# Cross-attention and gated feed-forward on one core: K's stacked rows laid out for two batches, and another ending for the last batch

## The reference

```python
x = x + attention(layernorm(x), ctx)     # 16 heads of depth 16, biases,
                                         # scores * 16**-0.5 / temperature[head], softmax
h = silu(n @ wg.T) * (n @ wu.T)          # n = layernorm(x), 768 hidden, int weights / 127
x = x + h @ wd.T
```

## Time and profile before

| | |
|---|---|
| runs | 410.18, 410.93 and 411.25 us, median 410.93 |
| the profiled execution | 409.33 us, of which 407.6 us are its span |
| busy | TensorE 89%, its weight loads 80%, VectorE 73%, ScalarE 63%, GpSimd 39% |
| mean granted TensorE clock | 0.975 |
| DMA packets | 61749, 34049 of them under 512 B; 37.68 MB |

### The profile page before, as it was taken

One profiled execution on the slowest core, in us unless ns is written; L12 is line 12 of the kernel. 1 busy time (PEld: TensorE's weight loads), 2 busy tenths in 40 slices (PEclk: granted clock), 3 DMA queues, 4 the chain that ended last, 5 costly groups with the idle time before them and its releaser, 6 DMA issues.

```text
span 407.6 us, 9738 instructions
## 1 busy us (share of the span) xinstructions
PE 363.9 (89%) x3398; PEld 326.9 (80%) x3398; DVE 298.2 (73%) x734; ACT 256.2 (63%) x564; POOL 158.7 (39%) x282
## 2 busy tenths in 40 slices
PE   0567578799999999999999999999998999998984
PEld 0566465688999899989999898999997988787984
DVE  6974657678878877787788778888777686745743
ACT  2353366577776767676777686767766675756442
POOL 3133313264434443343426263626353061613322
PEclk9979689999999999999999999999999999999989
DMA  6999595536523753184525591739137622010000
GB/s 174 294 101 155 76 157 88 87 76 123 101 65 77 141 118 78 33 161 110 112 58 89 124 157 32 141 53 159 26 84 83 113 31 81 15 42 2 27 27 27
DMA packets 61749, 37.68 MB, mean 92 GB/s; under 512 B 34049, under 2 KB 61185, under 8 KB 61697
## 3 DMA queue, kind: packets, MB, share of 16 engines
q1 hardware_dynamic: 61696, 36.99, 47.4%
HBM read 14.04 MB, written 4.19 MB: 45 GB/s over the span
## 4 chain that ended last, share of the span: by engine, by line
PE 67%; DMA 11%; SPq 6%; DVE 5%; ACT 4%; issue 3%; POOL 3%; ACTq 0%; DVEq 0%
PE ps_w L807 28%; DMA qs<-q 9%; PE ps_w L800 9%; PE ps_o L936 6%; PE ps_b L920 6%; PE ps_a L910 6%; SPq L395 5%; PE ps_w L792 5%; PE ps_w L819 4%; PE ps_w L840 3%; DMA ks<-k 1%; ACT probs L545 1%; DVE ks L695 1%; POOL hidT L463 1%; DMA probs<-wkT 1%
## 5 line engine op out<-in xcount | busy, mean ns | idle before, releaser
L463 POOL TENSOR_TENSOR hidT<-hid,hidT 128x256 fp32r<-128x256 f32 x80 | 58.9, 738 | 124.7 <-ACT hidT L538 124.7
L807 PE MATMUL ps_w<-xn2T,wg 128*128 128x256 f32 x384 | 103.0, 301 | 0.2 <-DVE xn2T L632 0.2
L807 PE MATMUL ps_w<-xn2T,wu 128*128 128x256 f32 x384 | 96.2, 282 | 0.0
L545 ACT ACTIVATE probs<-ps_b 120x512 f32<-120x512 f32 x128 | 76.0, 593 | 22.8 <-PE ps_b L920 22.5
L710 DVE TENSOR_REDUCE negmax<-ps_a 128x4 f32<-128x480 f32 x128 | 82.8, 648 | 8.7 <-PE ps_a L910 8.4
L807 PEld LDWEIGHTS ps_w<-xn2T,wg 128*128 128x128 f32 x384 | 72.9, 190 | 1.5 <-issue 0.5
L807 PEld LDWEIGHTS ps_w<-xn2T,wu 128*128 128x128 f32 x384 | 73.1, 190 | 0.0
L910 PE MATMUL ps_a<-ks,qs 96*128 96x120 bf16 x512 | 49.9, 222 | 12.0 <-DMA qs<-q 7.5
L556 ACT ACTIVATE tanh_g<-ps_w 128x256 f32<-128x256 f32 x96 | 36.8, 383 | 37.2 <-PE ps_w L807 35.9
L807 PE MATMUL ps_w<-wd,hidT 128*128 128x256 f32 x384 | 55.8, 293 | 3.0 <-POOL hidT L463 2.6
L920 PE MATMUL ps_b<-qs,ks 98*120 98x256 bf16 x256 | 50.6, 279 | 4.6 <-ACT probs L545 3.2
(11 more groups left out here) (93 smaller groups left out, 602.9 us busy)
## 6 DMA issues: line engine op xcount, KB each, us to landing
qs<-q SPq DMA_DIRECT2D x96, 128.0 KB, 4.5
ks<-k SPq DMA_DIRECT2D x96, 60.0 KB, 2.6
x_tok<-x SPq DMA_DIRECT2D x16, 256.0 KB, 4.5
x_res<-x SPq DMA_DIRECT2D x16, 256.0 KB, 4.6
out<-y SPq DMA_DIRECT2D x16, 256.0 KB, 2.5
ctx_raw<-ctx SPq DMA_DIRECT2D x16, 120.0 KB, 4.3
y<-wgT SPq DMA_DIRECT2D x2, 384.0 KB, 5.7
x<-wuT SPq DMA_DIRECT2D x2, 384.0 KB, 6.7
```

Of the source, the lines that this page charges most:

```text
L463: nc.gpsimd.tensor_tensor(hidT[:, 1, f], hid[:, f % 2], hidT[:, 0, f].bitcast(F32), ALU.subtract).then_inc(hid_lo, 1)
L545: nc.scalar.activation(probs[0:NKV, e % PROBS], ps_b[0:NKV], ACT.Exp).then_inc(exp_done, 1)
L807: last = nc.tensor.matmul(dst, lhsT, rhs, start=(start and k == 0), stop=(stop and k == len(terms) - 1), skip_group_check=True)
```

## The change

`ks` becomes two buffers, each for two batches side by side, and SP copies K's rows for both batches of a pair with the same six issues. VectorE's ones rows are set by GpSimd at its start. For the last batch VectorE makes the low parts of chunks 0 to 4 as well, and the output is stored in two halves, one after each output sum. The tables change with it: most entries by a few steps.

```diff
-        ks = [sb(f"ks{r}", [KS_ROWS + 2, H, NKV], BF16) for r in range(RING)]
+        ks = [sb(f"ks{r}", [KS_ROWS + 2, H, 2, NKV], BF16) for r in range(2)]
...
+def pair_count(pair):
+
+    return (pair // 2 + 1) * (6 * 16)
...
-            def stack(kind, n, part, t, dst, arrived, parts):
+            def stack(kind, n, part):
 
                 at_least(sp, b_full, count(n - RING, GROUPS, GROUPS))
                 sp.wait_ge((hi, mid, lowest)[part][kind], job_count(kind, 0, n))
-                src = t[:, part, :, n % 2] if kind == "k" else t[:, part]
+                if kind == "k":
+                    dst, src, arrived, parts = ks[n // 2 % 2], k3[:, part], ks_in[n // 2 % 2], K_PARTS
+                else:
+                    dst, src, arrived, parts = qs[n % RING], q3[:, part], qs_in[n % RING], Q_PARTS
                 for r in range(len(parts)):
                     if parts[r] == part:
-                        sp.dma_start(dst[n % RING][r * D:(r + 1) * D], src).then_inc(arrived[n % RING], 16)
+                        sp.dma_start(dst[r * D:(r + 1) * D], src).then_inc(arrived, 16)
...
                 for n, part in due("k rows", i, 3):
-                    stack("k", n, part, k3, ks, ks_in, K_PARTS)
+                    if n % 2 == 0:
+                        stack("k", n, part)
...
                 for n, _ in due("store", i):
-                    sp.wait_ge(emptied["down"], count(n, QT, QT))
-                    sp.dma_start(out[n].rearrange("(t p) c -> p t c", p=P), y[:, n % RING]).then_inc(stored[n % RING], 16)
+                    if n == NB - 1:
+                        for t in range(QT):
+                            sp.wait_ge(emptied["down"], count(n, QT, t + 1))
+                            sp.dma_start(out[n, t * P:(t + 1) * P], y[:, n % RING, t]).then_inc(last_stored, 16)
+                    else:
+                        sp.wait_ge(emptied["down"], count(n, QT, QT))
+                        sp.dma_start(out[n].rearrange("(t p) c -> p t c", p=P), y[:, n % RING]).then_inc(stored[n % RING], 16)
...
             pool.wait_ge(consts_done, 1)
+            for pair in range(2):
+                nc.gpsimd.memset(ks[pair][KS_ROWS:], 1.0).then_inc(k_ones_set, 1)
+                pool.wait_ge(k_ones_set, pair + 1)
...
                 for n, f in due("hid lo", i, FC - 1):
-                    hidden_lo(n, f)
+                    if n < NB - 1:
+                        hidden_lo(n, f)
...
-                for back in ((2, 1) if kind == "k" else (1,)):
-                    if n >= back:
-                        act.wait_ge(arrived[(n - back) % RING], slot_count(n - back, 1, 1) * (6 * 16))
+                if kind == "k" and n > 0:
+                    act.wait_ge(ks_in[(n // 2 - 1) % 2], pair_count(n // 2 - 1))
+                if kind == "q" and n > 0:
+                    act.wait_ge(qs_in[(n - 1) % RING], slot_count(n - 1, 1, 1) * (6 * 16))
...
-                if i == START["ones rows"]:
-                    for r in range(RING):
-                        last = nc.vector.memset(ks[r][KS_ROWS:], 1.0)
-                    last.then_inc(k_ones_set, 1)
...
+                for n, f in due("hid lo dve", i, FC - 1):
+                    if n == NB - 1:
+                        dve.wait_ge(hi["hid"], count(n, FC, f + 1))
+                        nc.vector.tensor_tensor(hidT[:, 1, f], hid[:, f % 2], hidT[:, 0, f].bitcast(F32), ALU.subtract).then_inc(hid_lo, 1)
```

More of the change, by code:

```diff
@@ L49 @@
     "attT lo": 70, "rsqrt2": 77, "x1": 78, "stats2": 79, "var2": 80, "norm2": 89, "normT2 hi": 89,
-    "normT2 lo": 91, "tanh": 94, "gate": 95, "hid": 96, "hid hi": 98, "hid lo": 100, "hid lo last": 118,
-    "y": 123, "store": 148,
+    "normT2 lo": 91, "tanh": 94, "gate": 95, "hid": 96, "hid hi": 98, "hid lo": 99, "hid lo dve": 103,
+    "hid lo last": 118, "y": 122, "store": 148,
 }
@@ L54 @@
     "rsum": 1, "k rows": 4, "q rows": 2, "exp": 4, "A": 4, "B": 4, "max": 4, "pv": 16, "pv copy": 15,
-    "tanh": 4, "gate": 4, "hid": 4, "hid hi": 4, "hid lo": 2, "y": 4,
+    "tanh": 4, "gate": 4, "hid": 4, "hid hi": 4, "hid lo dve": 4, "hid lo": 2, "y": 4,
 }
 START = {
-    "load wv": -96, "load wo": -44, "load bv": -116, "load bo": -21, "weight q": -72, "weight o": -25,
-    "weight v": -51, "ones rows": -133, "load wg": (-57, -51), "load wu": (-47, -45), "load wd": (-42, -40), "int hi": (-46, -29, -21),
-    "int lo": (-36, -25, -18), "squares": (-20, -19, -15, -14, -11, -9), "tell": -3, "sum": 2, "told": 7, "read": 63,
+    "load wv": -96, "load wo": -44, "load bv": -116, "load bo": 1, "weight q": -72, "weight o": -33,
+    "weight v": -54, "load wg": (-57, -51), "load wu": (-51, -45), "load wd": (-42, -40), "int hi": (-46, -29, -22), "int lo": (-36, -25, -18),
+    "squares": (-20, -19, -15, -14, -11, -5), "tell": -7, "sum": 2, "told": 8, "read": 63,
 }
 SHIFT = {
-    "A": {0: 5, 1: 2, 3: -1, 14: -1, 15: -1},
+    "A": {0: 5, 1: 2, 3: -1, 13: -2, 14: -1, 15: -1},
+    "B": {1: -4},
     "att": {0: -1},
@@ L117 @@
     "stats2": {0: -3},
-    "store": {0: -5, 2: 9, 3: 1, 13: -4, 14: -17, 15: -12},
+    "store": {0: -5, 2: 9, 3: 9, 13: -4, 14: -17, 15: -12},
     "tanh": {14: 1, 15: 21},
-    "v": {0: 4, 1: -7, 2: 16, 3: 5},
-    "var1": {0: -73, 1: -11, 2: -5, 3: -9, 13: -3, 14: 1, 15: 1},
+    "v": {0: 4, 1: -7, 2: 16, 3: 5, 15: 2},
+    "var1": {0: -73, 1: -11, 2: -7, 3: -9, 13: -6, 14: 1, 15: 1},
     "var2": {0: -3, 15: 2},
     "wo": {0: -1, 3: -2},
-    "x1": {0: -3},
-    "y": {0: -1, 13: -3, 14: 3, 15: 41},
+    "x1": {0: -3, 13: -1},
+    "y": {0: -1, 13: -3, 14: 3, 15: 44},
 }
-FIRST, LAST = -222, TURN * (BATCHES - 1) + 229
+FIRST, LAST = -205, TURN * (BATCHES - 1) + 232
 @lru_cache(None)
@@ L288, in build @@
         qs_in = [sem(f"qs_in{r}") for r in range(RING)]
-        ks_in = [sem(f"ks_in{r}") for r in range(RING)]
+        ks_in = [sem(f"ks_in{r}") for r in range(2)]
         shift_in = [sem(f"shift_in{r}") for r in range(RING)]
+        last_stored = sem("last_stored")
         stored = [sem(f"stored{r}") for r in range(RING)]
@@ L426, in step @@
                 for n, part in due("q rows", i, 3):
-                    stack("q", n, part, q3, qs, qs_in, Q_PARTS)
+                    stack("q", n, part)
                 for n, _ in due("store", i):
-                    sp.wait_ge(emptied["down"], count(n, QT, QT))
-                    sp.dma_start(out[n].rearrange("(t p) c -> p t c", p=P), y[:, n % RING]).then_inc(stored[n % RING], 16)
+                    if n == NB - 1:
[5 more added lines that the diff above has]
+                        sp.dma_start(out[n].rearrange("(t p) c -> p t c", p=P), y[:, n % RING]).then_inc(stored[n % RING], 16)
             for r in range(RING):
@@ L435, in _ @@
             for r in range(RING):
-                sp.wait_ge(stored[r], 16 * (1 + len(range(r, NB, RING))))
+                sp.wait_ge(stored[r], 16 * (1 + len(range(r, NB - 1, RING))))
+            sp.wait_ge(last_stored, 16 * QT)
         @block.gpsimd
@@ L910, in step @@
                         last = nc.tensor.matmul(ps_a[ga % 2][:, k * NKV:(k + 1) * NKV], qs[n % RING][0:KS_ROWS, h0 + k, qt * P:(qt + 1) * P],
-                                                ks[n % RING][0:KS_ROWS, h0 + k], start=True, stop=True)
+                                                ks[n // 2 % 2][0:KS_ROWS, h0 + k, n % 2], start=True, stop=True)
                     last.then_inc(a_full, 1)
@@ L919, in step @@
                     for k in range(HG):
-                        last = nc.tensor.matmul(ps_b[0:NKV, k * NQ:(k + 1) * NQ], ks[n % RING][:, gb * HG + k], qs[n % RING][:, gb * HG + k],
+                        last = nc.tensor.matmul(ps_b[0:NKV, k * NQ:(k + 1) * NQ], ks[n // 2 % 2][:, gb * HG + k, n % 2], qs[n % RING][:, gb * HG + k],
                                                 start=True, stop=True)
```

21 lines of the change are left out of this document (11 added, 10 removed), and 28 rows, old and new, of tables (LAG, SHIFT).

## The result

The change makes the kernel slower, not faster. The runs of the kernel after took 414.28 to 416.36 us, median 415.44, against a median of 410.56 us for the kernel before: a ratio of 1.0129 (1.0092 to 1.0165). On another chip, beside other kernels, it was 1.0091 (1.0063 to 1.0119), a median of 414.26 against 409.45 us. So it costs some 4 to 5 us, where 2.3 us less were forecast, and the time lies outside the range.

What follows compares the result with a forecast made beforehand. It took TensorE to bound the steady part, full from 100 to 200 us, with the loss at the beginning. Terms -2.1 - 0.5 + 0.5 - 1.5 + 0.4 + 0.2 + 1.1 - 0.4 gave -2.3 us: 408.6 us, range 405.5 to 412.0.

Steps and rivals of the forecast that it cites:

- The wait at 40.67: ScalarE's wait at the start for K rows copied out of `k3` goes: net -2.1 us (bounds 0 and -2.9).
- I cost them at nothing: Order moves on VectorE, ScalarE, loads and stores: zero, covered by a full TensorE; 5 us if Q rest became late.
- Bytes before batch 2's Q rows: Middle and lowest K rows put 180 KB more right ahead of those Q rows: +0.5 us (0 to 1.4).
- Batch 3: Its Q rows no longer stand behind six K rows on SP: -1.5 us (0 to -2.1).
- Even batches later: Lowest K row ahead of Q rows carries 60 KB more: batch 14 pays +0.4 us, all others +0.2.
- a sign that the prediction had named: Listed under what would show it wrong: waits for Q rows in the even batches over 1 us.
- The ones rows: At the start, memsets move from VectorE to GpSimd; VectorE's 5.7 us saving becomes 0.4 us as another chain arrives.
- Clock: Near 46 to 50 us, shorter TensorE idle time brings back some granted clock: -0.5 us (none, or -2).
- The tail: Last batch: VectorE's low parts +1.1 us (0.5 to 1.7), output stored in halves -0.4 (0 to -1).
- the clock coming back: Rival: TensorE keeps the upper level over 46 to 50 us, extra bytes cost nothing: 406.6 us; chance 0.17.
- the long memsets: Rival: GpSimd's memsets at the start take 1.56 ns an element, ending at 13.6 us: 414.0 us; chance 0.12.
- the mixture with a moved step late on VectorE: Rival: Q rest comes late behind an output sum that isn't ready: 412 to 414 us; chance 0.08.

Runs made afterwards that it cites:

- e1: Kernel before with K's rows in pairs and nothing else, VectorE's ones-row memsets now two of 3840 elements: 412.33 us, 1.0072.
- e14: Kernel after with ones rows filled late on GpSimd, last batch's low parts back on GpSimd and batch 0's `x_res` bias later: 409.83 us, 1.0005.
- e11: Kernel before with K's rows in pairs, ones rows late on GpSimd, batch 0's `x_res` bias later and last output in halves: 405.95 us, 0.9909.
- e17: e11's kernel once more on another chip, against the kernel before: 407.48 us, 0.9940.
- e16: e11's kernel with twenty useless matmuls ahead of TensorE's wait for batch 2's Q rows: 408.15 us, 0.9960 of the kernel before.
- e15: Kernel before with only batch 0's `x_res` bias moved behind the third part of K of batch 2 on GpSimd: 409.78 us, 0.9995.
- e9: Kernel after with only batch 0's `x_res` bias on GpSimd moved to a later step: 411.99 us, 1.0053 of the kernel before.
- e13: Kernel after, unchanged, measured once more on another chip: 414.26 us, 1.0091 of the kernel before.
- e5: Kernel before with its three ones-row memsets moved from VectorE's start to GpSimd behind the third part of batch 0's Q: 407.87 us, 0.9954.
- e6: e5 with K's rows in pairs besides: 408.92 us, 0.9976 of the kernel before.
- e12: e5 with batch 0's `x_res` bias later and the last output in halves, K's rows single: 407.17 us, 0.9934 of the kernel before.
- e18: e11's kernel with the changed START table alone: 407.38 us, 0.9950 of the kernel before.
- e7: Kernel after with its two GpSimd ones-row memsets moved from the start to behind the third part of batch 0's Q: 412.62 us, 1.0045.
- e8: Kernel after with twenty useless matmuls filling TensorE's wait before batch 2's scores: 413.30 us, 1.0088 of the kernel before.
- e3: Kernel after with the last batch's low parts back on GpSimd: 412.58 us, 1.0063 of the kernel before.

## Why the prediction was wrong

**What was right.** The two memsets on GpSimd, forecast at 3.2 us each and done at 8.2, from the timeline:

```profile
1.67 6.81 POOL L468 MEMSET ks<- 2x3840 bf16 x2
...
8.56 0.20 POOL L474 TENSOR_TENSOR minus_mean<-zero_col,meanvar 128x2 f32<-128x2 f32 x1
...
11.98 0.76 PE L815 MATMUL ps_w<-ctxT,wk 128*128 128x240 f32 x2
...
15.05 2.27 PE L823 MATMUL ps_w<-xn1T,wq 128*128 128x256 f32 x12 [0.18 <-DVE xn1T L655]
```

They took 3.30 and 3.47 us and were done at 8.49. The first K product came at 11.98 (forecast 11.7), and the rest of K at 15.82 (forecast 15.5). The factor of two of the Trainium skill, "GPSIMD Engine Reference", key points, does not hold for a memset: e1's row on VectorE is 3.26 us for the same 3840 elements, and the next one starts 4.00 us after it. The bytes are what counts, not the packets, in the main: 193 us of 16 engines with a third fewer packets, which agrees with the exemption for transfers from SBUF to SBUF in the Trainium skill, "DMA: Bandwidth & Descriptors", bandwidth section. The two rows under the earlier trace rows are no proof of it, though. At 88 us K rows were still under way (SP issued them until 87.2; 199 of the stretch's 303 packets are under 512 B). And the pairs' runs are of 960 B, not 480, as a part's four stretches of 240 B (two halves of the channels, two batches) now lie side by side: from 48 to 51 us of the kernel after only K rows move, 288 packets for 0.25 MB. Their 32.3% of 16 engines is 62 ns a KB, where it was 80. Over all of K's rows that would be some 7 us of the 193, and the profiles with pairs differ by more among themselves (189.5 to 198.5). The wait at 40.67 went, as the step said. The form of the tail was as forecast.

**The step that failed first: "I cost them at nothing".** The moves in the order were priced at zero, because "their cover is the work of a TensorE that is full". From batch 4's scores on the profiles bear that out, with e14 as fast as e11 and e17. They do not bear it out before, where the earlier trace rows showed TensorE busy two thirds of the time up to 60 us. There the order costs some 2 to 4 us (e14 against e16, e17 and e11), as much as any term of the sum, and its bound at the far end (5 us) was attached to the wrong place, Q rest in a dozen full batches.

**The second: "The wait at 40.67", -2.1 us.** The wait went, and its gain did not arrive. The rest of K of batch 2 came 1.20 us earlier (40.40, before 41.60) and not 2.1, as the rest of Q of batch 1 came 1.63 us later behind the check (37.08, before 35.45) and not 0.8. And what is late next was not asked. The lowest K row and the Q rows of batch 2 wait on SP for the third part of K on GpSimd, and ahead of that stand the bias of `x_res` of batch 0, which needs a load, and batch 3's normalization, which needs VectorE's statistics. With the K rows' wait gone, the statistics came 1.26 us earlier (47.08, then 45.82). But the load of `x_res` left SP 0.5 us later (40.53, before 39.99) and took 0.4 us longer, as it stands behind the Q rows of batch 1, and those behind the check of the integer weights. GpSimd's timeline, before and after:

```profile
46.23 1.41 POOL L489 TENSOR_TENSOR x_res<-x_res,bo_row 128x256 f32<-128x256 f32 x2 [8.04 <-DMA x_res<-x]
...
48.96 1.10 POOL L468 TENSOR_TENSOR k<-k_rest,k 128x480 bf16<-128x480 f32 x1
```

```profile
38.70 1.15 POOL L489 TENSOR_TENSOR q<-q_rest,q 128x512 bf16<-128x512 f32 x1 [1.33 <-ACT q L547]
...
47.21 1.43 POOL L511 TENSOR_TENSOR x_res<-x_res,bo_row 128x256 f32<-128x256 f32 x2 [7.37 <-DMA x_res<-x]
...
49.95 1.09 POOL L489 TENSOR_TENSOR k<-k_rest,k 128x480 bf16<-128x480 f32 x1
```

So K's third part came 1.0 us later, not 2 earlier. e15 and e9 show both sides of it: in the kernel before, the load's wait alone was worth nothing, in the changed one its removal comes with 0.4 to 0.8% (the lower value, against e13, is inside the intervals). Two chains of equal length stood at 47 us, and the change shortened one and lengthened the other.

**"Bytes before batch 2's Q rows", +0.5 us:** 1.4 us, the far bound; the last row needed 6.77 us instead of 5.38. The engines' gap before 48 us, on which the low value rested, lies ahead of K's late third part, and the doubled K row now leaves with the Q rows behind it.

**"Batch 3", -1.5 us:** the wait went (1.4 us in e5, none in e6), but it is not seen as a gain of the whole. **"Even batches later", +0.6 us,** were priced too low: their waits grow by 1.3 us from e5 to e6, and in the changed kernel TensorE's one wait after 300 us is 2.5 us where it was 1.8, a sign that the prediction had named. The pairs without anything else (e6 against e5, e11 against e12) come to +0.9 and -1.0 us, while the terms at 40.67 and of batch 3 promised 3.6, and all terms of the pairs together 3.0.

**"The ones rows", -0.4 us.** The start did gain: the first Q product is 2.5 us earlier. But 7 us later nothing is left of it, in VectorE's and TensorE's rows:

```profile
20.84 1.47 DVE L626 TENSOR_TENSOR wo<-probs,wo 128x512 fp32r<-128x512 f32 x1
...
22.57 0.86 DVE L662 SCALAR_TENSOR_TENSOR q_rest<-ps_w,bq_col,q 128x256 f32<-128x256 f32 x2
...
23.48 1.12 PE L842 MATMUL ps_w<-ident,xn 128*128 128x128 f32 x4 [4.72 <-DVE q_rest L662]
```

The weight of o, moved ahead, stands before batch 0's Q rest on VectorE, which comes at 22.57 where it came at 22.20. TensorE idles 4.7 us and goes on at the lower level: its four transposes take 1.12 us where they took 0.66. In e18, without the early memsets, the same move makes nothing late (Q rest at 20.95, in e17 21.12). The memsets themselves were priced well; that neither place at the start is a good one (e5, e7) was the thing to see.

**"Clock", -0.5 us:** the sign is wrong, the clock is lower from 42 to 56 us (0.50, before 0.63) and from 60 to 80 (0.66, before 1.00). By e8 this costs at most a part of the loss by itself. One rival, the clock coming back, fell with it.

**The tail, +1.1 and -0.4 us:** +0.6 and -1.2 in the profile. VectorE needs 1.25 us a chunk, not 1.36. The 1.0 us of the last matmuls is the clock level, which no term held.

The rival that ends on the other side, the long memsets (414.0), came near the measured time for a reason that was not the case. Nearest to what happened was the mixture with a moved step late on VectorE, which had 0.08 and 412 to 414 us; but the steps seen late stood behind the weight of o and the check, not behind an output sum, and by e18 these two moves cost little by themselves; and the second wait behind the one removed stood in no rival. What stays open is which entries of the batches' tables cost the 2 to 4 us, how much of that is the clock, and how much of e3's gain is the slow end.

## What to carry to other kernels

Before a removed wait is counted, look at every other engine's arrival at the same point, above all in-order queues that hold a wait of their own: where two chains end within a microsecond, the gain is what separates them. Here the reordering was free only in the stretch where the bounding engine is full; where it idles, each moved entry needs its own line in the sum. And work that is not needed soon, as the ones rows here, belongs in an idle stretch of an engine, not at the start, where the first steps of VectorE and of GpSimd were both awaited here.

## What the runs showed of the hardware

- A memset of 2 partitions by 3840 bf16 has a row of 3.29 to 3.47 us on GpSimd and of 3.26 on VectorE. But on VectorE the next memset starts 4.00 us later (e1; 2.01 us for 1920 elements before), on GpSimd 3.35 us later: 1.04 ns an element against 0.87. A VectorE memset costs over a fifth more than its row.
- Instructions of VectorE and GpSimd can grow when they run beside each other. VectorE's cast of `wk` took 0.79 us beside GpSimd's memset (0.43 before), and its subtraction for `wo` 1.47 us (0.69 before) beside GpSimd's third part of K, 1.28 us (1.10 elsewhere). A GpSimd operation of two elements, mostly 0.20 us, took 1.36 at 19.16 us, beside VectorE's low part of `wg` (1.81 for another such one beside it in the kernel before). Not each does: VectorE's subtraction for `wk`, beside the same memset as the cast, took 0.69 us as before.
- K's rows in runs of 960 B instead of 240 cost little less: 120 KB landed in 3.9 us at the median where 60 KB landed in 2.6, and the queue's total time is 189.5 to 198.5 us of 16 engines in the fourteen profiles with pairs and 193.2 to 198.0 in the six without.
- A clock held up by matmuls of no use (1.00 from 60 to 80 us) did not clearly shorten the runs when the engine waited for transfers there anyway (medians of 413.30 us in e8 and 414.26 in e13, 408.15 in e16 and 407.48 in e17, each pair on two chips).
- A dozen runs of one kernel spread over 3 to 6 us (e15: 408.3 to 411.4; e7: 408.3 to 414.2). Between two profiles of one kernel (e11, e17) the first loads' time on the path (4.22 or 5.31 us) and the granted clock from 20 to 40 us (0.83 or 1.00) both differed.
